# Two layers over a 10,000 x 10,000 matrix: where the slices of the moving matrix lie in the on-chip memory

## The reference

```
h  = item_feat @ W_item.T + b_item                    # 10000 x 128
b  = layernorm(x) @ W_user.T + b_user
x1 = x + relu(adj @ h + b)                            # first layer: reads all of adj, 400 MB
o  = lstm(layernorm(x1))                              # second layer: 10000 steps, hidden size 128
g  = argmax(o @ W_lin.T + b_lin)                      # 0 or 1 for each step
w  = g * o;  inc = cumsum(w)
out = x1 + 2*o + (inc - w) * fw_att + (inc[-1] - inc) * bw_att
```

## Time and profile before

| | |
|---|---|
| runs | 1430.08, 1429.75, 1426.78 us; median 1429.75 |
| profiled execution | 1429.61 us, of which the span is 1427.8 us |
| granted TensorE clock | 0.995 of full speed, mean over the span |
| first layer | 10.0 us to 1126 us; blocks 1 to 19 take about 54.6 us each |
| second layer | 1126 us to 1427.8 us |
| busy, share of the span | PE 98%, PEld 85%, DVE 89%, ACT 74%, POOL 15% |
| moved | 442.96 MB, 310 GB/s over the span |

### The profile page before, as it was taken

How to read it: one execution, slowest core, us unless ns; L and a number is a source line. 1 busy time by engine, 2 the same in 40 slices (tenths; PEclk the granted TensorE clock), 3 DMA queues, 4 the chain that set the end, 5 groups by cost and what they waited for, 6 DMA issues and landing times.

```text
span 1427.8 us, 26195 instructions
## 1 busy us (share of the span) xinstructions
PE 1401.8 (98%) x7438; PEld 1210.5 (85%) x7438; DVE 1273.0 (89%) x2102; ACT 1056.4 (74%) x1449; POOL 213.4 (15%) x189
## 2 busy tenths in 40 slices
PE   8999999999999999999999999999999999999995
PEld 7888888888888888888888888888888899999995
DVE  7999999999999999999999999999999766676667
ACT  5677787777877877877877877877877676556663
POOL 0000000001001001001001001001000132036776
PEclk9999999999999999999999999999999999999998
DMA  9999999999999999999999999999999303000003
GB/s 373 344 336 382 399 387 392 394 385 383 405 385 395 391 387 397 392 382 402 384 387 402 391 377 405 387 380 402 388 388 382 133 1 144 0 2 0 0 0 145
DMA packets 143466, 442.96 MB, mean 310 GB/s; under 512 B 23944, under 2 KB 43337, under 8 KB 143307
## 3 DMA queue, kind: packets, MB, share of 16 engines
q1 hardware_dynamic: 126048, 426.43, 76.7%
q10 hardware_dynamic: 17387, 16.14, 4.0%
HBM read 432.15 MB, written 10.36 MB: 310 GB/s over the span
## 4 chain that ended last, share of the span: by engine, by line
PE 93%; DVE 5%; ACT 0%; issue 0%; DMA 0%; POOL 0%; ACTq 0%; DVEq 0%
PE psG L882 24%; PE psG L883 24%; PE psG L884 24%; PE psZ L980 10%; PE psZ L966 3%; PE psZ L968 3%; PE psZ L970 3%; DVE a_lo L1201 2%; PE psZ L986 1%; PE psT L857 1%; PE psI L930 1%; DVE item_lo L1234 1%; DVE u L1516 1%; DVE u L1215 0%; PE psG L875 0%
## 5 line engine op out<-in xcount | busy, mean ns | idle before, releaser
L665 ACT ACTIVATE a_hi<-raw 128x1000 fp32r<-128x1000 f32 (+1 forms) x800 | 819.5, 1030 | 241.9 <-PE psG L884 212.7
L1201 DVE TENSOR_TENSOR a_lo<-raw,a_hi 128x1000 fp32r<-128x1000 f32 (+1 forms) x800 | 897.8, 1171 | 22.9 <-ACT a_hi L665 19.9
L882 PE MATMUL psG<-a_hi,item_hi 128*128 128x500 f32 x1560 | 611.3, 392 | 2.3 <-DVE a_lo L1201 1.4
L883 PE MATMUL psG<-a_lo,item_hi 128*128 128x500 f32 x1560 | 606.0, 388 | 0.0
L884 PE MATMUL psG<-a_hi,item_lo 128*128 128x500 f32 x1560 | 604.6, 388 | 0.0
L882 PEld LDWEIGHTS psG<-a_hi,item_hi 128*128 128x128 f32 x1560 | 293.5, 188 | 65.5 <-DVE a_lo L1201 3.5
L884 PEld LDWEIGHTS psG<-a_hi,item_lo 128*128 128x128 f32 x1560 | 293.1, 188 | 59.5
L883 PEld LDWEIGHTS psG<-a_lo,item_hi 128*128 128x128 f32 x1560 | 293.7, 188 | 55.5
L980 PE MATMUL psZ<-hist,wh 128*128 (+1 forms) x1264 | 167.1, 275 | 2.9 <-DVE hist L1354 2.2
L980 PEld LDWEIGHTS psZ<-hist,wh 128*128 128x128 f32 x1264 | 154.0, 191 | 3.8 <-issue 2.4
L466 POOL TENSOR_TENSOR row_terms<-var,minus_half 125x4 f32<-125x4 f32 x20 | 37.6, 1878 | 677.9 <-DVE var L1152 677.9
(11 more groups left out here) (186 smaller groups left out, 857.1 us busy)
## 6 DMA issues: line engine op xcount, KB each, us to landing
raw<-in_adj_main SPq DMA_DIRECT2D x760, 500.0 KB, 6.6
raw<-in_adj_main SPq DMA_DIRECT2D x40, 250.0 KB, 4.7
sq<-rstd_copy ACTq DMA_DIRECT2D x20, 250.0 KB, 7.0
u<-x_copy SPq DMA_DIRECT2D x1, 5000.0 KB, 14.4
x_copy<-x_rows SPq DMA_DIRECT2D x19, 250.0 KB, 7.2
sq<-rows_copy ACTq DMA_DIRECT2D x19, 250.0 KB, 5.3
un_bb<-rows_copy ACTq DMA_DIRECT2D x19, 250.0 KB, 7.6
u<-in_itemT SPq DMA_DIRECT2D x9, 512.0 KB, 8.0
```

The source lines that it names most:

```text
L665: nc.scalar.activation(a_hi[:, s % CUT, 0:n], raw[:, r % RAW, at:at + n], ACT.Copy)\
L882: pe.matmul(bank, w_hi, hi, start=(c == 0), stop=False)
L883: pe.matmul(bank, w_hi, lo, start=False, stop=False)
L1201: last = dve.tensor_tensor(a_lo[:, s % CUT, 0:m], raw[:, r % RAW, at:at + m], a_hi[:, s % CUT, 0:m].bitcast(f32), ALU.subtract)
```

## The change

Only the places of tiles change, and with them the shape of the access patterns of two steps.

- `a_hi` and `a_lo` become one tile, `a_both`. In it a chunk begins 512 elements (2048 bytes) behind the one before it in its half, not 500 (2000 bytes); a half begins 1012 elements (4048 bytes) behind the one before it, not 1000 (4000 bytes). The ring still has four halves.
- The first `hi` chunk begins 52 elements behind the start of `a_both`, the first `lo` chunk 4172 elements.
- ScalarE's copy (L665) and VectorE's subtraction (L1201) of a half therefore write and read two runs of 500 elements with a gap of 12 between them, where before they had one run of 1000.
- Seven small tensors of the layer norm are declared between `item_hi` and `item_lo`; `item_tail` and `inv_rows`, used in block 0 alone, become parts of `x1_rows`, which is unused there.

The addresses in the built program after: `item_hi` 68928, `item_lo` 109664, `raw` 150112, `a_both` 182112, so the first `hi` chunk is at 182320 and the first `lo` chunk at 198800. The remainders by 512 are 320 for `item_hi`, 96 for `item_lo`, 48 for the first `hi` chunk and 144 for the first `lo` chunk; 48 is 240 ahead of 320, counted round, and 144 is 48 ahead of 96. The tiles of the second layer that are declared behind `inv_rows` all move down by 512 bytes; `u` stays.

No instruction is added, removed or put in another place on any engine, and no wait changes.

```diff
+CHUNK, SLOT = 512, 1012
+HI_AT, LO_AT, BOTH = 52, 4172, 8232
...
-        inv_rows = sb("inv_rows", [2, P])
...
         item_hi = sb("item_hi", [P, (CH + 1) * HID], f32r, first)
-        item_tail = sb("item_tail", [P, STACKED], f32, first)
+        moments = sb("moments", [SW, SUB, 6], f32, first)
+        mean_sum = sb("mean_sum", [SW, SUB], f32, first)
...
+        rstd1 = sb("rstd1", [SW, SUB], f32, first)
         item_lo = sb("item_lo", [P, (CH + 1) * HID], f32r, first)
         raw = sb("raw", [P, RAW, MAXC * BW], f32, first)
-        a_hi = sb("a_hi", [P, CUT, HALF * BW], f32r, first)
-        a_lo = sb("a_lo", [P, CUT, HALF * BW], f32r, first)
+        a_both = sb("a_both", [P, BOTH], f32r, first)
...
+        item_tail = x1_rows[:, 2 * HID:2 * HID + STACKED]
+        inv_rows = x1_rows[0:2, 3 * HID:4 * HID]
...
+        def chunk(at, s, i):
+            a = at + s % CUT * SLOT + i * CHUNK
+            return a_both[:, a:a + BW]
+
+        def chunks(at, s, n=HALF):
+            if n == 1:
+                return chunk(at, s, 0)
+            a = at + s % CUT * SLOT
+            return a_both[:, a:a + n * CHUNK].rearrange("p (c k) -> p c k", k=CHUNK)[:, :, 0:BW]
+
+        def by_chunk(t, n):
+            return t.rearrange("p (c k) -> p c k", k=BW) if n > BW else t
...
-                nc.scalar.activation(a_hi[:, s % CUT, 0:n], raw[:, r % RAW, at:at + n], ACT.Copy)\
+                nc.scalar.activation(chunks(HI_AT, s, n // BW), by_chunk(raw[:, r % RAW, at:at + n], n), ACT.Copy)\
...
-                            hi = a_hi[:, s % CUT, i * BW:(i + 1) * BW]
-                            lo = a_lo[:, s % CUT, i * BW:(i + 1) * BW]
+                            hi = chunk(HI_AT, s, i)
+                            lo = chunk(LO_AT, s, i)
...
-                last = dve.tensor_tensor(a_lo[:, s % CUT, 0:m], raw[:, r % RAW, at:at + m],
-                                         a_hi[:, s % CUT, 0:m].bitcast(f32), ALU.subtract)
+                last = dve.tensor_tensor(chunks(LO_AT, s, m // BW), by_chunk(raw[:, r % RAW, at:at + m], m),
+                                         chunks(HI_AT, s, m // BW).bitcast(f32), ALU.subtract)
```

More of the change, by code:

```diff
@@ L148, in program @@
         item_hi = sb("item_hi", [P, (CH + 1) * HID], f32r, first)
-        item_tail = sb("item_tail", [P, STACKED], f32, first)
+        moments = sb("moments", [SW, SUB, 6], f32, first)
+        mean_sum = sb("mean_sum", [SW, SUB], f32, first)
+        mean_gap = sb("mean_gap", [SW, SUB], f32, first)
+        gap_sq = sb("gap_sq", [SW, SUB], f32, first)
+        spread = sb("spread", [SW, SUB], f32, first)
+        var = sb("var", [SW, SUB], f32, first)
+        rstd1 = sb("rstd1", [SW, SUB], f32, first)
         item_lo = sb("item_lo", [P, (CH + 1) * HID], f32r, first)
         raw = sb("raw", [P, RAW, MAXC * BW], f32, first)
-        a_hi = sb("a_hi", [P, CUT, HALF * BW], f32r, first)
-        a_lo = sb("a_lo", [P, CUT, HALF * BW], f32r, first)
+        a_both = sb("a_both", [P, BOTH], f32r, first)
         xb = sb("xb", [P, 2, BW], f32, first)
@@ L166, in program @@
         v = un_bb[:, 0:BW]
[L167 to L172, removed]
         row_terms = sb("row_terms", [SW, 2, SUB], f32, first)
         rstd, shift_rows = row_terms[:, 0, :], row_terms[:, 1, :]
-        rstd1 = sb("rstd1", [SW, SUB], f32, first)
         factors = sq
@@ L875, in body @@
                                 last = pe.matmul(bank, item_hi[0:STACKED, c * HID:(c + 1) * HID],
-                                                 a_hi[0:STACKED, s % CUT, i * BW:(i + 1) * BW], start=False, stop=True)
+                                                 chunk(HI_AT, s, i)[0:STACKED], start=False, stop=True)
                                 continue
-                            hi = a_hi[:, s % CUT, i * BW:(i + 1) * BW]
-                            lo = a_lo[:, s % CUT, i * BW:(i + 1) * BW]
+                            hi = chunk(HI_AT, s, i)
+                            lo = chunk(LO_AT, s, i)
                             w_hi = item_hi[:, c * HID:(c + 1) * HID]
@@ L1200, in split_lo @@
                 m = n - BW if tail else n
-                last = dve.tensor_tensor(a_lo[:, s % CUT, 0:m], raw[:, r % RAW, at:at + m],
-                                         a_hi[:, s % CUT, 0:m].bitcast(f32), ALU.subtract)
+                last = dve.tensor_tensor(chunks(LO_AT, s, m // BW), by_chunk(raw[:, r % RAW, at:at + m], m),
+                                         chunks(HI_AT, s, m // BW).bitcast(f32), ALU.subtract)
                 if tail:
                     mid = slice(STACK[1], STACK[1] + TAIL)
-                    last = dve.tensor_tensor(a_hi[mid, s % CUT, m:n], raw[mid, r % RAW, at + m:at + n],
-                                             a_hi[mid, s % CUT, m:n].bitcast(f32), ALU.subtract)
+                    short = chunk(HI_AT, s, 1)[mid]
+                    last = dve.tensor_tensor(short, raw[mid, r % RAW, at + m:at + n], short.bitcast(f32),
+                                             ALU.subtract)
                 last.then_inc(lo_ready, 1)
```

## The result

| | median of the runs | ratio to before, 95% interval |
|---|---|---|
| before | 1429.75 us | |
| after | 1435.62 us | 1.0046 [1.0033, 1.0058] |

The change makes the kernel 0.46% slower (five runs of each). I had forecast 1418.6 us with a range from 1402 to 1434: wrong in sign, and outside the range.

The account below looks back on a forecast made before the run. TensorE was taken to bound blocks 1 to 19. Cheaper products there were to save 11.1 us, all other terms 0, so 1429.7 - 11.1 = 1418.6 us, range 1402 to 1434 (the forecast's own 1410 to 1425).

Parts of the forecast that it names:

- What bounds the kernel: Blocks 1 to 19: TensorE sets their length, busy 54.60 of 54.60 us; block 0 gains nothing from a faster product.
- The differences come from TensorE alone: Ring places, 0.69 against 0.67 us a chunk: claimed to come from how moving chunks lie to weights, not other engines.
- I take for all four new distances the 0.670 of their neighbours: Blocks 1 to 19, 1482 chunks: each falls from 0.6775 to 0.670 us, saving 7.5 ns, 11.1 us in all.
- the three cheap places: Old ring's places (3,1), (0,0), (0,1), distances 240/48, 64/384, 16/336: 0.670 us a chunk; the five others average 0.682.
- Only the remainder by 512 counts: Moving chunks and weights: shifts by 512 bytes cost nothing, so the second layer's moved tiles were put at 0.
- The gap of the weights "at nothing": `item_lo` lies 288 instead of 320 behind `item_hi`, changing `lo`'s distance to `item_hi`; costed at nothing.
- Two runs instead of one at 0: VectorE's subtraction and ScalarE's copy: a second run costs 0; other end 6.0 us more per block on VectorE.
- Cover and loads: Blocks 1 to 19: VectorE and loads keep up; at 27.5 ns saved per chunk, about 0.2 us per block lost.
- rival 3: The ring's four halves: new distances are dear, 0.685 to 0.69 us a chunk, 11 to 18.5 us slower; chance 0.14.
- rival 1: TensorE's products: nothing changes, four distances average about what eight did; 1427 to 1432 us, middle 1429; chance 0.20.

## Why the prediction was wrong, point by point

- *What bounds the kernel*: right. TensorE sets blocks 1 to 19, block 0 and the second layer did not move, and what a product gained or lost came through to the time, in both directions, save for the waits at 220.0 ns.
- *The differences come from TensorE alone*: right: with the other engines silent, TensorE alone gives both kernels to 0.1 ns a product.
- *"I take for all four new distances the 0.670 of their neighbours"*: this is the step that failed. The term was -11.1 us and measured +6.2. A chunk takes 0.682 us, not 0.670. The reading behind it, that the time between two starts belongs to the distance of that product, does not hold: the three cheap places are not cheap when held (226.7, 225.9, 226.7 ns), and one place costs 220 or 229 by what ran before it. What a whole repeat of the pattern sums to is real; how it is shared out over the places is not theirs.
- *Only the remainder by 512 counts*: it was not refuted; weights stepping by 512 bytes cost what weights at one address cost (228.9 ns), and the series of 32 single distances even repeats by 256 at 14 of its 16 places (not at 0, which ran first and whose second to sixth product still took 415 to 419 ns, nor at 224, 227.8 against 226.7 ns).
- *The gap of the weights "at nothing"*: wrong. Taken first, it costs 0.16 us a block, 3 of the 6 us by the blocks of one trace (the medians say 1.7 us), with the tiles that moved behind it; with the new steps at 64/384 it gains 0.10 us.
- *Two runs instead of one at 0*: right, 1195 and 1041 ns.
- *Cover and loads*: right for this change, 1.0 us of waits in all. For faster products the loss of some tenths of a us per block did appear, but larger than worked out: about 0.4 at 0.660 a chunk, where I had 0.2 at 0.650.
- *The rivals.* The third had the sign and nearly the price (0.682 us against 0.685 to 0.69), but its reason, that a held distance is a dear one, is not what happens: held, the four average what the eight did. That it came near is luck. The reason I gave for rival 1, a delay booked on a later product and places cheap by what ran before them, was the right mechanism, at 0.20; but I let it end at "no change", as if averages had to agree. They agree only within the scatter, 0.64 ns or some 3 us for one standard deviation, and before stood on the good side of it; with that measured first, slower would have been the likelier side. The measured 1435.62 us lies between the two rivals: rival 1 ended at 1432, and rival 3 by its own price begins at 1441, so the range up to 1434 left out all of rival 3 and not only its dear half.

*A rule of the Trainium skill.* The Trainium skill, "SBUF — State Buffer", section "Who interferes with whom", says that PE never waits on anyone. The five sets that ran both ways agree with that, to 0.1 ns a product, with all other engines silent or at work. From this and from the two independent read ports that the Trainium skill, "TensorE: Matmul & The Clock Gate", Part 2, gives TensorE, the prediction had also drawn a rival by which places are worth nothing. That the traces do not bear out: held streams range from 220.0 to 240.0 ns.

*Still open*: what inside TensorE makes the rhythm. It does not need a full weight load (32 columns cost as much), moving the weights alone changes it, and so does moving both. Also open is why block 0 takes 74.8 to 75.1 us in three of the variants and 76.6 to 77.1 in the others; with one trace of each kernel, it may differ from run to run.

## What to carry to other kernels

A trace that repeats to the nanosecond looks like a table of costs per address, and need not be one: take the mean over a whole period, and ask what the scatter of such means is before claiming a gain from a new layout. A stream of products that is the only bound can be rebuilt with nothing but its instructions and addresses; here that gave whole kernels to 0.1 ns a product, in one run for many layouts, once whole blocks were rebuilt and not only a few turns of the ring. The layout that won had every moving chunk at one and the same remainder, and found its cheapest rhythm again after each break. Most such layouts are no better than the rest: 2 of the 256 held pairs gave 220.0 ns, and they had to be searched for.

## What the hardware showed that I had not expected

- Products of 500 columns one behind another, with a weight load each, settled at 220.0, 223.3, 226.7 or 228.9 ns at 31 of 32 single distances (227.8 at the other). 500 columns at 2.4 GHz are 208.3 ns; no held stream came below 220.0.
- Which one it is can hang on six products that ran before, and it then held to the end of the 24 that followed (220.0 against 228.9 ns over the last twelve).
- In the kernel before, 226 ns was taken for what a product costs. 5.6 ns of it, 2.5%, could be had by placement alone.
